# Norms in finer beats, and other places for the norms of the second MLP's first steps

## The reference

```python
# 1: layer norm, scale and shift; attention of 16 heads over 4 key heads, sparse mask
h = (x - mu) * rsqrt(var + 1e-5) * (1 + scale) + shift
x = x + attention0(h) @ Wo.T
# 2: RMS norm; attention of 8 heads over 1 key head; RMS norm; gated MLP, 2048 wide
x = x + attention1(n1(x)) @ Wo.T
x = x + (silu(n2(x) @ Wg.T) * (n2(x) @ Wu.T)) @ Wd.T
# 3: norms of queries and keys; attention of 16 heads; MLP with a GELU, 2048 wide
x = x + attn(_ln(x) * (scale1 + 1.0) + shift1) * gamma1
h = _gelu_tanh((_ln(x) * (scale2 + 1.0) + shift2) @ Wfc1.T + bfc1)
x = x + (h @ Wfc2.T + bfc2) * gamma2
# 4: eight experts of 64 features each, GELU; layer norm, scale and shift; SiLU, linear
y = einsum(gelu(einsum(x, W1) + b1), W2) + b2
x = x + silu(_layernorm(y, ln_g, ln_b) * (1.0 + scale) + shift) @ out_W + out_b
```

## Time and profile before

| | us |
|---|---|
| median of 3 runs | 2766.51 |
| lowest, highest run | 2765.05, 2771.02 |
| profiled execution, its own time | 2766.66 |
| its span (first to last recorded instruction) | 2764.9 |
| TensorE (PE) busy | 2543.1 |
| VectorE (DVE) busy | 1228.8 |
| ScalarE (ACT) busy | 1162.3 |
| GpSimd (POOL) busy | 304.3 |

### The profile page before, as it was taken

One profiled execution on the slowest core, in us unless ns is written; L12 is line 12 of the kernel. 1 busy time (PEld: TensorE's weight loads), 2 busy tenths in 40 slices (PEclk: granted clock), 3 DMA queues, 4 the chain that ended last, 5 costly groups with the idle time before them and its releaser, 6 DMA issues.

```text
span 2764.9 us, 31998 instructions
## 1 busy us (share of the span) xinstructions
PE 2543.1 (92%) x13000; PEld 1525.8 (55%) x13000; DVE 1228.8 (44%) x2482; ACT 1162.3 (42%) x2451; POOL 304.3 (11%) x264
## 2 busy tenths in 40 slices
PE   5678999899999999999999979999998888999998
PEld 1234444445555467788877534444444456777733
DVE  1136546444344643433433243636456644444333
ACT  0246566554344532111113154746566644222274
POOL 3134213112102010000001010101001010000021
PEclk8889999999999999999999979999999899999999
DMA  8100000000000000100001000000000010000001
GB/s 296 39 1 1 1 1 7 18 8 9 1 8 24 23 24 1 46 24 23 23 6 62 15 1 1 1 1 1 1 1 31 16 46 16 31 16 1 1 16 46
DMA packets 37555, 61.20 MB, mean 22 GB/s; under 512 B 5232, under 2 KB 18336, under 8 KB 36896
## 3 DMA queue, kind: packets, MB, share of 16 engines
q1 hardware_dynamic: 35056, 52.84, 5.7%
q0 software_dynamic: 2352, 6.32, 0.6%
HBM read 52.86 MB, written 4.19 MB: 21 GB/s over the span
## 4 chain that ended last, share of the span: by engine, by line
PE 75%; DVE 11%; ACT 9%; DMA 2%; POOL 2%; issue 1%; SPq 0%; DVEq 0%; POOLq 0%; ACTq 0%
PE banks L924 26%; PE banks L299 21%; PE banks L567 8%; PE banks L559 7%; PE banks L583 5%; DVE sb_Pr L639 2%; PE banks L593 2%; DVE sb_x L994 1%; PE banks L395 1%; DVE sb_PT L646 1%; ACT sb_hidH L950 1%; DVE sb_hidL L981 1%; ACT sb_Pr L668 1%; PE banks L335 1%; PE banks L476 1%
## 5 line engine op out<-in xcount | busy, mean ns | idle before, releaser
L924 PE MATMUL banks<-sb_HH,sb_Ws 128*128 128x512 f32 x1536 | 492.9, 395 | 7.0 <-DVE sb_Ws L967 5.5
L668 ACT ACTIVATE sb_Pr<-sb_Pr,sb_nmax 128x512 f32<-128x512 f32 (+3 forms) x512 | 326.1, 638 | 125.1 <-DVE sb_nmax L639 123.3
L924 PE MATMUL banks<-sb_hidH,sb_Ws 128*128 128x512 f32 x1024 | 352.6, 405 | 23.7 <-DVE sb_x L994 17.5
L567 PEld LDWEIGHTS banks<-sb_ident,sb_Pr 128*128 128x128 f32 x2176 | 250.1, 146 | 217.0 <-issue 96.1
L567 PE MATMUL banks<-sb_ident,sb_Pr 128*128 128x128 f32 x2176 | 324.2, 290 | 29.8 <-ACT sb_PT L673 20.8
L559 PE MATMUL banks<-sb_R 32*128 32x512 f32 (+4 forms) x1280 | 308.8, 609 | 38.9 <-DVE sb_nmax L639 26.3
L639 DVE CUSTOM_DVE_ANT_0 sb_Pr<-banks,sb_bias 128x512 f32<-128x512 f32 (+3 forms) x512 | 292.1, 581 | 104.3 <-PE banks L559 103.5
L646 DVE COPY sb_PT<-banks 128x512 f32<-128x512 f32 (+3 forms) x320 | 195.1, 610 | 319.1 <-PE banks L567 316.0
L924 PEld LDWEIGHTS banks<-sb_HH,sb_Ws 128*128 128x128 f32 x1536 | 290.7, 189 | 72.3 <-issue 11.9
L673 ACT ACTIVATE sb_PT<-banks 128x512 f32<-128x512 f32 (+3 forms) x320 | 169.0, 528 | 337.4 <-PE banks L567 336.5
L924 PE MATMUL banks<-sb_HL,sb_Ws 128*128 128x512 f32 x768 | 300.9, 392 | 0.0
(11 more groups left out here) (155 smaller groups left out, 2650.1 us busy)
## 6 DMA issues: line engine op xcount, KB each, us to landing
sb_staged<-in_L_cond_Wfc SPq DMA_DIRECT2D x16, 512.0 KB, 4.3
sb_WM<-in_L_cond_Wada SPq DMA_DIRECT2D x6, 1024.0 KB, 4.9
sb_x<-in_x SPq DMA_DIRECT2D x4, 1024.0 KB, 13.6
sb_staged<-in_L_cond_Wg SPq DMA_DIRECT2D x8, 512.0 KB, 3.4
sb_staged<-in_L_cond_Wu SPq DMA_DIRECT2D x8, 512.0 KB, 4.3
sb_staged<-in_L_cond_Wd SPq DMA_DIRECT2D x8, 512.0 KB, 3.5
out_x<-sb_x SPq DMA_DIRECT2D x4, 1024.0 KB, 4.5
sb_WM<-in_L_cond_W_ada SPq DMA_DIRECT2D x2, 1024.0 KB, 13.8
```

The costliest lines, as they stand in the source:

```text
L567: mm = e.transpose(bank[:, j * P:(j + 1) * P], k.Pr[:, n % 6, j * P:(j + 1) * P], k.ident[:])
L668: ins = e.activation(prob, prob if s.biased else k.bank(n % 4)[:, 0:s.width(u)], ACT.Exp, bias=s.stat(k, k.nmax, b, u), scale=-1.0 if s.bi ...
L924: mm = e.matmul(bank, lhsT, rhs, start=i == 0, stop=i == len(mats) - 1)
```

## The change

`SideNorm.beats` gives a norm in smaller beats. Before, squares stood with mean and centres; scales, shifts and extras were one beat, in which scale and shift of a tile alternate. Now squares, scales, shifts and extras have a beat each, and one more empty beat stands ahead of mean and of variance. A norm with a mean has 11 beats in place of 7 (norm2, norm2b), or 10 without extras. An RMS norm has 6 in place of 5: one more empty beat ahead of the variance. In the second MLP's first steps the streams have other bounds, and `pair2` of batch 1 goes from there to the end of `attention2`. No instruction is added or taken away. Inside one norm the order on each engine is the same; what changes is which other work stands between.

```diff
-        tail = [adds, [], [("pe", "var", 0), ("act", "log", 0), ("dve" if s.root else "act", "inverse", 0)]]
+        tail = [adds, [], [], [("pe", "var", 0), ("act", "log", 0), ("dve" if s.root else "act", "inverse", 0)]]
         if s.rms:
             return [squares] + tail + [scales]
-        ends = [op for c in range(C) for op in (("dve", "scale", c), ("act", "shift", c))]
+        ends = [[("dve", "scale", c) for c in range(C)], [("act", "shift", c) for c in range(C)]]
         if s.extra:
-            ends += [("act", "extra", c) for c in range(C)]
-        return [[("pool", "xsum", i) for i in range(3)], [],
-                [("pe", "mean", 0)] + [op for c in range(C) for op in (("dve", "centre", c), ("act", "square", c))]] \
-            + tail + [ends]
+            ends.append([("act", "extra", c) for c in range(C)])
+        return [[("pool", "xsum", i) for i in range(3)], [], [], [("pe", "mean", 0)] + [("dve", "centre", c) for c in range(C)],
+                squares] + tail + ends
...
-                           closing=[[], first[0], [], first[1]])
-        hidden2 = fold(parts, (0, 2, beats((pair2, 1))), (0, 4, beats((post2, 3))), (2, 3, mlp2.split(1)),
-                       (start[1], start[3], beats((norm2b, 2), (pair2, 2))),
-                       (start[3], start[5], beats((norm2b, 3), (pair2, 3))))
+                           closing=[sum(beats((pair2, 1)), []), first[0], [], first[1]])
+        hidden2 = fold(parts, (0, 3, beats((post2, 3))), (2, 3, mlp2.split(1)),
+                       (0, start[3] - 2, beats((norm2b, 2))), (start[3] - 2, start[3], beats((pair2, 2))),
+                       (start[3], start[5] - 2, beats((norm2b, 3))), (start[5] - 2, start[5], beats((pair2, 3))))
```

## The result

The changed kernel takes 2819.9 us (median of 4 runs, 2819.24 to 2821.23) where the kernel before took 2765.78 beside it. The ratio is 1.0195 (95% interval 1.0177 to 1.0213): 54 us more. The forecast was 2757, with 2772 as the upper end.

What follows compares the result with a forecast made beforehand. The prediction took TensorE, busy 92% of the span, as the bound, so only its waits and low-clock stretches could shrink. Its terms summed to 9.7 us saved, from 2766.66 to 2757.0 us, range 2745 to 2772.

Runs made afterwards that it cites:

- e1: The new beats alone, with closing points and second MLP's streams of the kernel before: ratio to that kernel 1.0177, 49 us slower.
- e4: The kernel before with only the queries' and keys' norm (qk2) of batches 1 to 3 at its new points: ratio 1.0144, 40 us slower.
- e5: The kernel before with only qk2's second sum, logarithm, exponential and first spread (batches 1 to 3) at their new points: ratio 1.0072, 20 us slower.
- e3: The changed kernel with only qk2 of batches 1 to 3 back at its old points: ratio to the kernel before 1.0044, 12 us slower.
- e11: The same kernel as e3, run again for a second trace: ratio to the kernel before 1.0037, profiled execution 2782.8 us.
- e10: New streams and closing points, new beats only for RMS norms and norm3, plus products of ones in two waits: ratio to the kernel before 0.9923.

## What to carry to other kernels

Where beats are spread evenly over a list, a change in the length of one stage moves every stage in the list, and by different amounts. Check each pair of producer and consumer in it, above all in the stages that the diff does not touch, and count what TensorE has to do between them against the latency of the chain. In a kernel that is 92% TensorE, price a gap not by its length but with the low clock behind it, which at the 4.19 us gaps here was three to eight times as long as the gap itself. The granted clock alone moved the same work by 12 and 18 us from one execution to another, so a trace of one execution must be read beside the ratio of many.

## What the runs showed of the hardware

- A wait of 4.19 us of TensorE, with 92% load around it, was accompanied and followed by 10.2 to 13.7 us of granted clock at the lower of its two levels, twelve times in four kernels (the changed one, e1, e4 and e5), and then by up to 20.5 more where eight narrow spreads with small waits followed. Filled with 6.96 us of products of ones, it was followed by none, 6.8 or 3.4 us, these some 9 us later; cut to 1.85 us, by none or 6.8. The length of a wait does not tell by itself: one of 7.04 us in the kernel before had 6.8 us (0.81 over 18 us), one of 6.77 in the changed kernel 13.7.
- Two executions of the same program, e3 and e11, differed by 18 us, and TensorE's busy time by 17.6 (2542.2 and 2559.8): nearly all of it is the clock. Filled waits at two places (e10) did not shorten the whole.
- In the norms with an exponential, and in those of queries and keys, logarithm and exponential each had a table load of 1.28 us ahead every time, 3.9 us for both with the two activations. The Trainium skill, "ScalarE: Activation LUTs", section "Table sets: the hidden batching unit", says that one table set holds both and that a logarithm followed by an exponential takes one load. The traces here have two, at L409 and L413 as at L222 and L226. With one load the waits of 4.19 us would be some 1.3 us shorter, by an estimate from the 1.28; no run here tries it.
